# Five untyped graph layers: the own term and the bias are built while the fp32 products run, and two VectorE operations end a sum

## The reference, cut to what matters

```python
def _gin_layer(h, src, dst, W, b, e, num_nodes):
    agg = segment_sum(h[src], dst)
    z = (1.0 + e) * h + agg
    return relu(z @ W + b)
# five of them (W1, b1, then Ws[i], bs[i]; e = eps[i]), then log_softmax(h, axis=1)
```

## Time and profile before

| | |
|---|---|
| median of three runs | 2041.11 us (2037.31 to 2041.81) |
| profiled execution | 2040.93 us, its span 2039.1 us |
| mean granted TensorE clock | 0.975 of full speed |
| busy in the span | TensorE matmuls 1897.2 us (93%), weight loads 900.4 us, VectorE 799.1 us, ScalarE 625.9 us, GpSimd 7.9 us |
| the five layers | from 1274.66 us to about 1873 us of the span |
| matmuls of a product tile | 8 records, 3.43 to 3.46 us |
| aggregation of a tile | 24 matmuls, 5.18 us |

### The profile page before, as it was taken

The page is one execution under the profiler, slowest core; times in us unless marked ns, Lnnn a source line. Parts: engine busy times, 40 slices in busy tenths (PEclk is TensorE's granted clock), DMA queues, the critical chain, the costliest instruction groups (busy, mean ns, idle before and its releaser), DMA issues.

```text
span 2039.1 us, 23800 instructions
## 1 busy us (share of the span) xinstructions
PE 1897.2 (93%) x7966; PEld 900.4 (44%) x7978; DVE 799.1 (39%) x1978; ACT 625.9 (31%) x1200; POOL 7.9 (0%) x27
## 2 busy tenths in 40 slices
PE   3888888699999899999999999999999999987998
PEld 2555555453333434444444444444444444433443
DVE  4777777334011261110112222354444444484122
ACT  1545454324764042111121010132232323274000
POOL 1000000000000000000000000000000000000000
PEclk9999999789999969999999999999999999998999
DMA  5999988831000141100000110800000000021011
GB/s 135 232 231 240 227 201 198 286 146 37 1 1 0 62 135 81 42 1 0 21 0 31 42 42 26 334 1 5 22 6 21 6 21 16 1 68 56 21 52 41
DMA packets 47380, 157.55 MB, mean 77 GB/s; under 512 B 9316, under 2 KB 11260, under 8 KB 38816
## 3 DMA queue, kind: packets, MB, share of 16 engines
q1 hardware_dynamic: 42160, 142.27, 24.0%
q10 hardware_dynamic: 5104, 13.78, 1.8%
HBM read 120.38 MB, written 35.65 MB: 77 GB/s over the span
## 4 chain that ended last, share of the span: by engine, by line
PE 79%; DVE 7%; ACT 4%; DVEq 3%; issue 3%; DMA 2%; another core or an unknown queue 1%; ACTq 1%
PE psum L1208 29%; PE psum L1194 29%; PE psum L1426 6%; PE psum L1277 3%; PE psum L1330 2%; PE psum L1377 2%; DVE hs L594 2%; PE psum L1112 2%; PE psum L1144 1%; DVE hs L596 1%; DVE hs L595 1%; DVEq L596 1%; PE psum L1143 1%; DMA hs<-in_L_gnn_basis 1%
## 5 line engine op out<-in xcount | busy, mean ns | idle before, releaser
L1208 PE MATMUL psum<-hs,adj 128*128 128x512 f16 x2880 | 643.1, 380 | 0.8 <-DVE hs L701 0.8
L1194 PE MATMUL psum<-wb,xt 128*128 128x512 f32 x1152 | 508.4, 599 | 15.5 <-DVE hs L829 13.4
L1208 PEld LDWEIGHTS psum<-hs,adj 128*128 128x128 f16 x2880 | 280.0, 98 | 354.1 <-issue 37.3
L1194 PEld LDWEIGHTS psum<-wb,xt 128*128 128x128 f32 x1152 | 218.2, 192 | 283.8 <-issue 281.7
L983 ACT ACTIVATE adj<-hs,pbias 128x512 f32<-128x512 f32 x216 | 134.5, 708 | 86.1 <-PE psum L1277 86.1
L1144 PE MATMUL psum<-hs 128*128 128x192 f32 x636 | 157.2, 329 | 0.0
L1016 ACT ACTIVATE ua<-ua 128x512 f32<-128x512 f32 x60 | 37.8, 631 | 335.4 <-DVE ua L843 187.7
L594 DVE TENSOR_SCALAR hs<-hs 128x128 f32<-128x128 f16 x318 | 89.7, 282 | 86.9 <-issue 48.8
L1426 PE MATMUL psum<-hs,adj 128*128 128x512 f32 x288 | 123.8, 592 | 0.0
L780 DVE TENSOR_TENSOR vt<-psum,adj 128x512 f32<-128x512 f32 x24 | 16.6, 692 | 271.9 <-PE psum L1194 271.9
L1143 PE MATMUL psum<-hs 128*128 128x384 f16 x318 | 106.5, 335 | 14.3 <-DVE hs L596 7.1
(11 more groups left out here) (216 smaller groups left out, 1508.7 us busy)
## 6 DMA issues: line engine op xcount, KB each, us to landing
hs<-in_L_gnn_basis SPq DMA_DIRECT2D x38, 960.0 KB, 9.3
adj<-in_L_gnn_basis SPq DMA_DIRECT2D x26, 960.0 KB, 9.7
aw_scratch<-xt ACTq DMA_DIRECT2D x12, 768.0 KB, 6.0
adj<-aw_scratch SPq DMA_DIRECT2D x1, 9216.0 KB, 38.2
x_scratch<-adj SPq DMA_DIRECT2D x24, 256.0 KB, 2.1
hs<-x_scratch SPq DMA_DIRECT2D x24, 256.0 KB, 2.6
ts_scratch<-adj SPq DMA_DIRECT2D x1, 4608.0 KB, 21.4
as_scratch<-adj SPq DMA_DIRECT2D x1, 4608.0 KB, 32.5
```

The costliest lines, as they stand in the source:

```text
L1194: x = pe.matmul(psum[:, bank, :], xt[:, i, k, :], w[:, k, :], start=first and k == 0, stop=last and k == 3)
L1208: x = pe.matmul(psum[:, i % 2 + (4 * half if own else 0), :], adj[:, m, j, P * i:P * i + P], hs[:, t, half, j, :], start=n == 1 or (own an ...
```

## The change

The own term with the bias is computed in the stage of the products, straight from the fp32 PSUM bank: `own(i) = u * (1 + e) + bias`, written over `xt[:, i]`, the transposed tile that the products of tile i have just read. The sum is then two operations: high bank times scale plus own(i), and low bank times (scale / 4096) plus that, straight into `ua`. Two 128x1 constants are made behind `scale(...)`. VectorE's wait for the bias moves ahead of the products' loop. The semaphore `v_pre` goes; what waited for it waits for `acc_read` (ScalarE's relu) or `u_lo` (the bias loads on the SP queue).

```diff
@@ -225,7 +225,7 @@
         m_ps, m_cp = sem("m_ps"), sem("m_cp")
         o_ps, o_read = sem("o_ps"), sem("o_read")
         relu_ready = sem("relu_ready")
-        v_pre, v_ready = sem("v_pre"), sem("v_ready")
+        v_ready = sem("v_ready")
         t_ps, t_cp = sem("t_ps"), sem("t_cp")
         var_ready, std_ready = sem("var_ready"), sem("std_ready")
         y_ready, y_out = sem("y_ready"), [sem(f"y_out{k}") for k in range(2)]
@@ -429,11 +429,11 @@
             for l in range(2, 5):
                 sp.wait_ge(u_ps, tick(1 + l, NT - 1))
                 gin_weights(l)
-                sp.wait_ge(v_pre, tick(V_OF[1 + l] - 1, NT - 1))
+                sp.wait_ge(u_lo, tick(1 + l, NT - 1))
                 gin_bias(l)
             sp.wait_ge(u_ps, tick(6, NT - 1))
             sp.dma_start(wb[:, 0, :, :], ins["L3_gnn_weight"].rearrange("(k p) n -> p k n", p=P)).then_inc(gin_in[5], 16)
-            sp.wait_ge(v_pre, tick(V_OF[6] - 1, NT - 1))
+            sp.wait_ge(u_lo, tick(6, NT - 1))
             bias(0, 2, ins["L3_gnn_bias"])
             norm_tiles(2, 2, xs_dram[1], xs_dram[2])
 
@@ -800,6 +800,10 @@
 
             kit = kits[2]
 
+            def own(i):
+
+                return xt[:, i, :, :].rearrange("p k n -> p (k n)")
+
             def log_softmax_end(i):
 
                 v, st = kit["yb"][:, i % 2, :], lnst[:, i % 2, :]
@@ -823,25 +827,24 @@
             for l in range(5):
                 r = 3 + l
                 scale(520.0 if l == 0 else None)
+                step(dve.tensor_scalar(scl[:, 7:8], scl[:, 1:2], 1.0 / LO_BY, None, ALU.mult))
+                step(dve.tensor_scalar(scl[:, 2:3], epsc[:, l:l + 1], 1.0, None, ALU.add))
+                dve.wait_ge(bb_in[r % 2], 16 * BB_COUNT[r])
                 for i in range(NT):
                     dve.wait_ge(u_hi, tick(r, i))
+                    dve.scalar_tensor_tensor(own(i), psum[:, 2 + i % 2, :], scl[:, 2:3], kit["bb"][:, r % 2, :], ALU.mult, ALU.add)
                     step(dve.scalar_tensor_tensor(vt[:, :], psum[:, 2 + i % 2, :], scl[:, 0:1], hs[:, 0, 0, i, :], ALU.mult, ALU.subtract))
                     dve.tensor_scalar(hs[:, 0, 1, i, :], vt[:, :], LO_BY, None, ALU.mult).then_inc(u_lo, 1)
                     dve.wait_ge(u_lo, tick(r, i))
-                dve.wait_ge(bb_in[r % 2], 16 * BB_COUNT[r])
-                step(dve.tensor_scalar(scl[:, 2:3], epsc[:, l:l + 1], 1.0, None, ALU.add))
                 for i in range(NT):
 
-                    step(dve.scalar_tensor_tensor(vt[:, :], hs[:, 0, 1, i, :], 1.0 / LO_BY, hs[:, 0, 0, i, :], ALU.mult, ALU.add))
                     dve.wait_ge(acc_ps, tick(r, i))
-                    step(dve.scalar_tensor_tensor(vt[:, :], vt[:, :], scl[:, 2:3], psum[:, i % 2, :], ALU.mult, ALU.add))
-                    dve.scalar_tensor_tensor(vt[:, :], psum[:, 4 + i % 2, :], 1.0 / LO_BY, vt[:, :], ALU.mult, ALU.add).then_inc(acc_read, 1)
-                    dve.wait_ge(acc_read, tick(r, i))
+                    step(dve.scalar_tensor_tensor(vt[:, :], psum[:, i % 2, :], scl[:, 1:2], own(i), ALU.mult, ALU.add))
                     if i >= 2 and l < 4:
                         dve.wait_ge(t_ps, tick(r, i - 2))
                         dve.wait_ge(v_ready, tick(V_OF[r], i - 2))
-                    dve.scalar_tensor_tensor(ua[:, i % 2, :], vt[:, :], scl[:, 1:2], kit["bb"][:, r % 2, :], ALU.mult, ALU.add).then_inc(v_pre, 1)
-                    dve.wait_ge(v_pre, tick(V_OF[r] - 1, i))
+                    dve.scalar_tensor_tensor(ua[:, i % 2, :], psum[:, 4 + i % 2, :], scl[:, 7:8], vt[:, :], ALU.mult, ALU.add).then_inc(acc_read, 1)
+                    dve.wait_ge(acc_read, tick(r, i))
                     if l == 4:
                         step(dve.tensor_scalar(ua[:, i % 2, :], ua[:, i % 2, :], 0.0, None, ALU.max))
                         dve.tensor_reduce(sml[:, i % 2, 0:1], ua[:, i % 2, :], AX.X, ALU.max, negate=True).then_inc(lsm_neg, 1)
@@ -1009,10 +1012,7 @@
 
             def relu(r, i):
 
-                if r == 1:
-                    act.wait_ge(acc_read, tick(r, i))
-                else:
-                    act.wait_ge(v_pre, tick(V_OF[r] - 1, i))
+                act.wait_ge(acc_read, tick(r, i))
                 act.activation(ua[:, i % 2, :], ua[:, i % 2, :], ACT.Relu).then_inc(relu_ready, 1)
                 act.wait_ge(relu_ready, tick(V_OF[r], i))
                 act.activation(kits[kit_of[r]]["mt"][:, i % 2, :, :].rearrange("p k n -> p (k n)"), ua[:, i % 2, :], ACT.Square,
```

## The result

| | before | changed |
|---|---|---|
| median | 2041.12 us (8 runs, 2037.31 to 2041.84) | 2049.0 us (8 runs, 2046.11 to 2053.49) |
| profiled execution, span | 2040.93, 2039.1 us | 2050.08, 2048.2 us |
| mean granted clock | 0.975 | 0.969 |
| VectorE busy | 799.1 us | 758.9 us |

The ratio is 1.0043, with a 95% interval of 1.0032 to 1.0054: slower by 7.9 us, where +1.3 on the median was forecast (2042.4) and 2046.5 was the upper end. VectorE does 40 us less, and the kernel is slower.

What follows compares the result with a forecast made beforehand. TensorE, 93% busy, was taken as the bound, with its waits at layer heads and in layer 7 deciding. 2.7 + 3.5 - 8.1 + 3.4 = +1.5 us on 2040.93 gave 2042.4 us, range 2036.5 to 2046.5.

Steps and rivals of the forecast that it cites:

- Term 1: Product stages: the own term is hidden except for tile 0, +0.67 us at each head of layers 4 to 7, +2.7 us.
- Term 2: Layer 3's head: VectorE waits for a bias load landing 6.6 us after issue; with the own term +3.5 us.
- Term 3: Layer 7: two operations leave the sum, shortening the loop and the wait behind aggregation 4, -8.1 us.
- Term 4: Layers 4 to 7: longer head waits bring two clock falls in four, 1.7 us each, +3.4 us (ends 0 and 9).
- A: Product tiles 2 and 3, layers 4 to 7: clock falls at nearly every head, 6 to 9 us, total 2046; chance 0.15.
- C: Layer 7 gains only the steady 2.9 us because another wait holds its first tiles, total 2047.6 us; chance 0.1.
- D: Layer ends: the shorter sum lets ScalarE convert tile 0 earlier, each of four gaining 2 x 0.73 us; chance 0.03.
- B: Layer 3's bias lands in time (3.2 us) and the clock holds, 2036 to 2038 us; chance 0.1.

Runs made afterwards that it cites:

- Experiment 6: The changed kernel with the biases of layers 3 and 4 loaded earlier, ahead of the last tile's store and layer 4's matrix: 2048.26 us, ratio 1.004.
- experiment 10: The kernel before with the new form (own term, bias wait, two-operation sum) in layer 7 alone: 2031.27 us, ratio 0.9954.
- experiment 11: The kernel before with the sum ended by two operations, own term and bias still made in the aggregation stage: 2037.37 us, ratio 0.9981.
- experiment 3: The kernel before with one more 0.67 us VectorE operation ahead of tile 0's L828 in layers 4 to 7: 2054.25 us, ratio 1.0064.
- experiment 4: The kernel before with an added half-width VectorE operation (256 columns) ahead of tile 0's L828 in layers 4 to 7: 2048.28 us, ratio 1.0037.
- experiment 1: The changed kernel with the own terms of tiles 0 and 1 made ahead of ScalarE's copy in layers 4 to 7: 2035.72 us, ratio 0.9977.
- experiment 7: The changed kernel with biases loaded early and own terms of tiles 0 and 1 ahead of ScalarE's copy in all five layers: 2034.2 us, ratio 0.9971.
- experiment 9: The kernel before with two unused fp32 filler matmuls on TensorE at each of the five layer heads: 2037.78 us, ratio 0.9983.

## Why the prediction was wrong

**Term 1, the own term.** Right in place and size: hidden behind ScalarE in every tile but the first, +0.67 to +0.69 a head. No product stage waited for VectorE after its first row.

**Term 2, the bias.** Right: the load landed 6.7 us after its issue, TensorE waited 6.17 us (6.2 forecast), the head was 3.5 us longer. Experiment 6 shows that the load's company made it late: issued earlier and ahead of the 1 MB load it lands in 3.2 us. Whether the matrix ahead of it decided, or the large load that is issued 2.7 us behind it, no run separates. The 2.6 us of the Trainium skill ("DMA: Bandwidth & Descriptors", two cost components), an estimate by a fit that the page gives for transfers issued from GpSimd, is not what this load from the SP queue took, in either place. Its rule on completion (queues, rings and completion order) agrees with 6.7 us behind 1 MB, but no run tests it against two loads that share the DMA engines.

**Term 3, layer 7.** Right, -8.4 us for -8.1: 22.9 and 68.4 us were forecast for the transposes behind aggregations 4 and 11, counted from the first sum; they came at 1816.72 - 1793.78 = 22.9 and at 68.2. Experiments 10 and 11 confirm both halves of the argument.

**Term 4, the clock.** Here it failed. "I take two falls in the four, at 1.7 each: +3.4 us" was 10.5 us: four falls, three of them 2.9 us and more. Two errors of about the same size.

The number: two falls too few, 3.4 us at the prediction's price. It had one fall in five waits of 2.67 us and one after 4.53 us, and nothing between the two. All profiles without filler at the heads give this together for layers 4 to 7 (layer 3 fell in each):

| wait before the products | heads | falls |
|---|---|---|
| 2.60 to 2.68 us | 22 | 3 |
| 3.06 us | 4 | 3 |
| 3.33 to 3.36 us | 14 | 13 |

From 2.67 to 3.36 us a fall thus went from the exception to the rule.

The price: 1.7 us was taken, by the 1.5 us of the one row at a head, where the stretch at half speed was short; the four cost 2.6 on average, 3.7 us more in all. The earlier trace rows had a sign of more. The fall after the 4.53 us wait cost 2.25 us in the aggregation and 0.45 in the transposes ahead of it (1.08 for 0.63), 2.7 together, near the 2.9 that came. The prediction priced it at the 2.25 alone, and took that as the end of the range.

With 10.5 in place of 3.4 the sum is +8.6 on the profiled execution's 2040.93, 2049.5 us, against a measured median of 2049.0.

**The rivals.** A is what happened, with its mechanism and place; its chance was put at 15%, and its price too low. Its own working gave 2046 us from four falls on, and even its upper end (9 us of falls, 2048.0 us) lay 1.5 us short. The range did not cover its own rivals: 2046.5 lies below that end of A and below C's 2047.6. C and D did not come: layer 7 gave all of its gain, and the ends of layers none (experiment 11). Nor did B: the load took 6.7 us and the clock fell four times. Experiment 6 made B's first half true by moving the load, and gained nothing that can be told.

**What stays open.** Layer 3 fell in all 11 profiles without filler at its head, after waits of 2.60 to 6.17 us, and lost the same 1.5 to 1.6 us after 2.67 as after 6.17 (2.8 in experiment 6, after 3.36); why is open. So is why layer 7 held after 3.36 us in experiment 10. Whether falls are chained from head to head is not shown. For it: the changed kernel and experiment 3, with nearly the same waits at layers 4 to 7, gave the same list of lengths; and the one head that held after 3.36 us had a head without a fall before it, the 13 others one with a fall. Against it: layer 5 in experiment 4 and layer 7 in experiments 1 and 7 fell though the head before had held, and experiment 6 gave another list at the same waits (37.41 and 37.49 us in layers 3 and 4).

## What to carry to other kernels

Where TensorE waits at a regular place, price a longer wait twice: by itself, and by every matmul behind it that then runs at half speed; take the price from the dearest fall anywhere in the trace, with all work that ran slow in it, and reckon with a fall at every repeat of the loop, not at some. Put work that has its inputs early (here the own term, whose product lay in PSUM for 3 us and more) ahead of the hand-over that everybody waits for; to put it behind L837, after that hand-over, was not tried. Make a change only where its gain lies: the new form gained in layer 7 and cost at the other heads, and in layer 7 alone it took 9.2 us off the kernel before (experiment 10), where in all five layers it added 7.9. One profile of a kernel is one draw of its clock, so its count of falls is no rate. A cheap test tells the clock from contention: fill the wait with matmuls that nobody uses.

## What the runs showed of the hardware that was not expected

0.67 us of VectorE work at four places cost 14.3 us (experiment 3), more than five times itself. A gain on the critical path can be eaten at once: 2.8 us less waiting at layer 3 left the time where it was (experiment 6), as the falls at layers 3 and 4 became 2.5 us longer. A fall can come when the wait is over: in layer 4 of the changed kernel the clock was at full speed for all of the 3.36 us and fell 1.1 us into the products. And matmuls that compute nothing of use made the kernel before 3.7 us faster (experiment 9).
